# A two-layer kernel's schedule: two lead-in experts moved into scan pairs 0 and 2, totals split, four more pairs summed by DMA, the last norm on VectorE

## What is computed

```python
# layer 0, feed-forward: 8 experts, every token through every expert, weights of the best two
h = gelu(einsum('te,ieh->tih', xf, w1) + b1)          # 128 -> 512, 8 experts
out = einsum('tih,ihe->tie', h, w2) + b2              # 512 -> 128
x = x + gb * sum(out * weights[..., None], axis=1)
# layer 1, attention-like part: a state-space scan, 16 states, 256 channels
dA = exp(dt_t[:, :, None] * A[None])
h = dA * h + (dt_t * xv_t)[:, :, None] * B_t[:, None, :]
y_t = einsum('bdn,bn->bd', h, C_t)                    # sum over the 16 states
x = x + ga * ((y * silu(z)) @ W_out.T)
# layer 1, feed-forward: a linear map by FFT, folded into one 128x128 matrix
x = x + gb * real(ifft(fft(layernorm(x)...) @ w)) + bias
```

## Time and profile before

| | us |
|---|---|
| median of 3 runs (lowest, highest) | 599.6 (598.94, 604.6) |
| the profiled execution, its own time | 605.89 |
| its span in the profile | 603.9 |
| busy: PE, DVE, ACT, POOL | 484.5, 429.1, 341.8, 348.0 |
| lead-in pair -12 to the first scan product | about 165 to 265.77 |
| scan pairs 0 to 31, first to last scan product | 265.77 to 577.64 |

### The profile page before, as it was taken

How to read it: one execution, slowest core, us unless ns; L and a number is a source line. 1 busy time by engine, 2 the same in 40 slices (tenths; PEclk the granted TensorE clock), 3 DMA queues, 4 the chain that set the end, 5 groups by cost and what they waited for, 6 DMA issues and landing times.

```text
span 603.9 us, 6833 instructions
## 1 busy us (share of the span) xinstructions
PE 484.5 (80%) x2346; PEld 337.3 (56%) x2346; DVE 429.1 (71%) x723; ACT 341.8 (57%) x455; POOL 348.0 (58%) x248
## 2 busy tenths in 40 slices
PE   3869867679989999989879979889888397677672
PEld 3457545344578887667666767656757243233231
DVE  4766897964534324059898799997998966987951
ACT  0531443224454655589998999979999255343100
POOL 3214977766432132315597667988487955567443
PEclk9986999979999999999999999999999588888796
DMA  8700000000000000301857655658627511211000
GB/s 292 274 1 0 1 1 1 2 0 0 1 0 2 1 2 0 142 1 46 198 115 151 158 137 141 145 117 207 144 74 171 122 54 53 71 69 35 17 0 18
DMA packets 15010, 44.75 MB, mean 74 GB/s; under 512 B 2240, under 2 KB 7744, under 8 KB 12544
## 3 DMA queue, kind: packets, MB, share of 16 engines
q0 software_dynamic: 2448, 17.83, 14.6%
q1 hardware_dynamic: 11952, 25.57, 12.5%
q10 hardware_dynamic: 576, 0.92, 0.5%
HBM read 25.31 MB, written 1.18 MB: 44 GB/s over the span
## 4 chain that ended last, share of the span: by engine, by line
PE 39%; DVE 28%; ACT 11%; POOL 10%; issue 7%; DMA 4%; ACTq 0%; POOLq 0%; DVEq 0%
PE pO L1219 8%; PE pY L1309 6%; DVE Hs L763 6%; DVE S L658 5%; DVE pCT L750 4%; PE pY L1266 3%; POOL ZS L383 3%; DMA Acc<-ZS 3%; PE pH L1207 3%; DVE pH L657 3%; ACT gel L961 3%; ACT dA L973 2%; PE pH L1209 2%; PE pH L1208 2%; POOL ln_x L353 2%
## 5 line engine op out<-in xcount | busy, mean ns | idle before, releaser
L1219 PEld LDWEIGHTS pO<-w_e,gel 128*128 128x128 f32 x1024 | 122.1, 192 | 13.9 <-issue 8.7
L1219 PE MATMUL pO<-w_e,gel 128*128 128x128 f32 x1024 | 124.7, 276 | 1.2 <-DVE X L734 1.0
L763 DVE TENSOR_TENSOR_SCAN Hs<-dA,HL,pCT 128x512 f32<-128x512 f32 x96 | 117.7, 1267 | 7.4 <-POOL Zev L383 3.7
L961 ACT ACTIVATE gel<-pH,b_e 128x512 f32<-128x512 f32 x128 | 86.1, 687 | 40.0 <-PE pH L1209 39.2
L383 POOL TENSOR_TENSOR ZS<-Hs,Crow 128x1024 f32<-128x1024 f32 x32 | 76.7, 2398 | 42.5 <-DVE Hs L763 42.5
L973 ACT ACTIVATE dA<-dt,a_neg 128x512 f32<-128x512 f32 x128 | 81.8, 710 | 15.8 <-DVE Hs L763 15.6
L750 DVE TENSOR_TENSOR pCT<-u,pB 128x1024 f32<-128x1024 f32 x64 | 78.3, 1224 | 16.8 <-PE pB L1291 15.8
L1207 PE MATMUL pH<-h2h,w_e1h 128*128 128x512 f32 x128 | 57.6, 450 | 21.1 <-ACT gel L961 20.1
L383 POOL TENSOR_TENSOR Zev<-Hs,Crow 128x1024 f32<-128x1024 f32 x26 | 62.5, 2408 | 17.3 <-DVE Hs L763 11.7
L734 DVE SCALAR_TENSOR_TENSOR X<-pO,wts,X 128x128 f32<-128x128 f32 x128 | 35.9, 342 | 42.1 <-PE pO L1219 42.0
L439 POOL TENSOR_TENSOR ZA<-Qsb,S 128x1024 f32<-128x1024 f32 x16 | 38.0, 2373 | 35.0 <-DVE S L658 32.7
(11 more groups left out here) (223 smaller groups left out, 882.8 us busy)
## 6 DMA issues: line engine op xcount, KB each, us to landing
Crow<-c_rows SPq DMA_DIRECT2D x32, 512.0 KB, 4.1
Acc<-ZS POOLq DMA_DIRECT2D x10, 1024.0 KB, 8.8
Acc<-Zev POOLq DMA_DIRECT2D x7, 1024.0 KB, 8.4
w_e<-in_w_e SPq DMA_DIRECT2D x2, 2048.0 KB, 10.6
X<-in_x SPq DMA_DIRECT2D x4, 256.0 KB, 7.4
out<-h2T SPq DMA_DIRECT2D x4, 256.0 KB, 2.5
S<-in_w_mod ACTq DMA_DIRECT2D x2, 384.0 KB, 4.9
w_cx<-in_conv_row SPq DMA_DIRECT2D x1, 512.0 KB, 9.5
```

What stands on the lines that cost most here:

```text
L763: vec.tensor_tensor_scan(Hs[:, 2 * o + d, 0:w], dA[:, 4 * (p % 2) + 2 * o + d, 0:w], pU[:, d, 0:w], HL[:, d, n:n + 1] if c else 0.0, ALU.m ...
L961: nc.scalar.activation(gel[:, n % NG, 0:w], pH[n % 2][:, 0:w], ACT.Gelu_apprx_tanh, bias=b_e1[:, NK * e + k:NK * e + k + 1]).then_inc(s["m ...
L1219: ins = mm(pO[:, j * P:(j + 1) * P], gel[:, n % NG, j * P:(j + 1) * P], w_e2[:, NK * (g % E) + k, :], start=(k == 0 and j == 0), stop=(k = ...
```

## The change

- **Experts.** A table gives the number of experts of each pair. Pairs -4 and -2 have none, pairs 0 and 2 have two. So expert 8 goes from pair -4 to -3, 9 from -3 to -1, 10 and 11 from -2 and -1 to pair 0, 12 from 0 to 1, 13 and 14 from 1 and 2 to pair 2; from expert 15 (pair 3) on nothing moves. The second expert of a pair runs whole after place B; its predecessor's `moe_acc` then stands at the end of the pair on DVE.
- **Sums.** DMA addition now runs to pair 23 (`TOT = 24`), so pairs 20 to 23 are added by DMA, chunk 2's gate is POOL's, and the Acc matmuls go. PE totals only chunk 3.
- **Split totals.** `total(p, o)` adds one half; half 0 comes ahead of place A and half 1 behind `row_b(2p+2)`.
- **Spare products.** `fill(n)` is n matmuls of 128x512 in the free bank pY0 whose result nobody reads: two in pair 20, four in pair 23, four and one in the last norm.
- **Last norm.** The last of the norms has its four multiplications on DVE and not on POOL.

```diff
 AHEAD = 12
+COUNTS = {-4: 0, -2: 0, 0: 2, 2: 2}
-ALONE = (NL * E - AHEAD) // 2 * 2
+EXPERTS = {p: [] for p in range(-AHEAD - 1, NL * NP + 1)}
+for p in range(-AHEAD, NL * NP):
+    g0 = sum(len(e) for e in EXPERTS.values())
+    EXPERTS[p] = list(range(g0, min(g0 + COUNTS.get(p, 1), NL * E)))
+ALONE = max(p for p in EXPERTS if EXPERTS[p]) + 1
+TOT = (ALONE + NP - 1) // NP * NP
...
         def alone(p):
-            return p >= ALONE
+            return p >= TOT
...
-                          ("end", "bias", last), ("mid", "ln_stats", last),
-                          ("A", "ln_turn", last, 2), ("A", "fft", last)):
+                          ("end", "bias", last), ("mid", "ln_last", last), ("A", "fill", 4),
+                          ("A", "ln_turn", last, 2), ("A", "fill", 1), ("A", "fft", last)):
...
+            def ln_last(c):
+                ln_stats(c)
+                vec.wait_ge(s["ln_rstd"], NC + 1)
+                vec.wait_ge(s["ln_tr"], L[0] - 1)
+                for j in range(blocks(c)):
+                    ins = vec.tensor_scalar(ln_x[:, j, :], rows_of(X, c)[:, j, :], ln_mv[:, j, 0:1], ln_rs[:, j:j + 1],
+                                            ALU.subtract, ALU.mult)
+                ins.then_inc(s["ln_xn"], 1)
...
+                free = ALONE <= p < TOT
+                if ALONE < p < NL * NP:
+                    total(p - 1, 0)
+                if free and not any(at == "A" and stage in mine for at, stage, *_ in stages):
+                    fill(2)
                 run(p, stages, "A")
                 if not moe and 0 <= 2 * p + 2 < NL * NS:
                     row_b(2 * p + 2)
-                if 0 < p < NL * NP:
-                    total(p - 1)
+                if ALONE < p < NL * NP:
+                    total(p - 1, 1)
+                if free and not any(at in ("B", "C") and stage in mine for at, stage, *_ in stages):
+                    fill(2)
...
+                for h in EXPERTS[p][1:]:
+                    for k in range(NK):
+                        up(h, k)
+                    for k in range(NK):
+                        down(h, k)
                 run(p, stages, "C")
...
+            def fill(n):
+                pe.wait_ge(s[held[2][0]], held[2][1])
+                warm(pY0, n)
```

More of the change, by code:

```diff
@@ L217, in totals @@
         def totals(p):
-            return p + 1 - ALONE
+            return p + 1 - TOT
         def summed(c):
-            return NP * (c + 1) <= ALONE
+            return NP * (c + 1) <= TOT
         def sums(p):
-            return len([q for q in range(min(p + 1, ALONE)) if q % 2 == p % 2 and q % NP])
+            return len([q for q in range(min(p + 1, TOT)) if q % 2 == p % 2 and q % NP])
         def col(n):
@@ L344, in _, with ln @@
             L = [0]
-            def ln(c):
+            def ln(c, last=False):
                 J = blocks(c)
@@ L368, in output @@
                 part = slice(2 * o, 2 * o + 2)
-                if p >= ALONE + 2:
+                if p >= TOT + 2:
                     Z = [Zev, ZS][p % 2][:, part, 0:w]
@@ L506, in run @@
                 for at, stage, c, *k in stages:
-                    if (at in ("B", "C", "end")) == last and stage in ("ln_stats", "rows", "route", "gate", "bias"):
-                        {"ln_stats": ln, "rows": rows, "route": route, "gate": gate, "bias": bias}[stage](c)
+                    if (at in ("B", "C", "end")) == last and stage in ("ln_stats", "ln_last", "rows", "route", "gate", "bias"):
+                        {"ln_stats": ln, "ln_last": lambda c: ln(c, True), "rows": rows, "route": route, "gate": gate, "bias": bias}[stage](c)
             for p, stages in later_stages():
@@ L793, in run @@
                         continue
-                    if stage in ("ln_stats", "step", "gate", "tail_x"):
-                        {"ln_stats": ln_stats, "step": step, "gate": gate, "tail_x": tail_x}[stage](c)
+                    if stage in ("ln_stats", "ln_last", "step", "gate", "tail_x"):
+                        {"ln_stats": ln_stats, "ln_last": ln_last, "step": step, "gate": gate, "tail_x": tail_x}[stage](c)
                     elif stage in ("route", "weigh", "fft"):
@@ L804, in _ @@
                     scans(2 * p)
-                if 0 < g <= NL * E:
-                    moe_acc(g - 1)
+                for g in EXPERTS.get(p - 1, [])[-1:]:
+                    moe_acc(g)
                 run(p, stages, False)
@@ L810, in _ @@
                     scans(2 * p + 1)
+                for g in EXPERTS[p][:-1]:
+                    moe_acc(g)
                 run(p, stages, True)
@@ L997, in _ @@
                 run(p, stages, "AB")
+                for g in EXPERTS[p][1:]:
+                    hidden(g, range(NK))
                 run(p, stages, "C")
@@ L1223, in pair @@
             def pair(p, stages):
-                g = p + AHEAD
-                moe = 0 <= g < NL * E
+                moe = bool(EXPERTS[p])
+                g = EXPERTS[p][0] if moe else None
                 if moe:
@@ L1337, in _ @@
             mine = {"ln_turn": lambda c, which, b: ln(c, b), "route": route, "turn": turn, "weigh": weigh, "x_part": x_part,
-                    "rows": rows, "dt_part": dt_part, "z_part": z_part, "total": total, "project": project, "fft": fft}
+                    "rows": rows, "dt_part": dt_part, "z_part": z_part, "total": totals_of, "project": project, "fft": fft,
+                    "fill": lambda n, b: fill(n)}
             def run(p, stages, places):
```

47 lines of the change are left out of this document (23 added, 24 removed).

## The result

| | before | after |
|---|---|---|
| median, us (4 runs each, taken together) | 601.12 | 609.93 |
| lowest, highest | 598.94, 604.6 | 608.02, 611.16 |
| ratio after to before, 95% interval | | 1.0139 [1.0094, 1.0183] |
| profiled execution, its span | 605.89, 603.9 | 611.16, 609.1 |

The change makes the kernel 1.4% slower, 8.8 us between the medians. (The ratio is not the quotient of the two medians, which is 1.0147; before was also measured afresh beside the experiments, with medians of 602.03, 602.19 and 602.08, so a difference between two kernels that were not measured together is uncertain by about 1 us.) The profiled execution of before lies 4.8 above its median and that of after 1.2 above, so the two traces differ by 5.3 only. I keep both accounts: the traces say where the time is, the medians how much it is.

A forecast was written before the change was run, and what follows sets the result against it. No single engine bounds it: PE in the lead-in, DVE, ACT and PE nearly level in scan pairs, a serial chain at the end. +6.7 + 2.5 - 0.7 + 1.3 - 3.4 = +6.4 on 599.6 gives 606.0 us, range 597.0 to 611.5.

The forecast's parts named there:

- pair -2 emptied: Lead-in: without its expert, pair -2 shrinks and the first row_b comes 5.7 us sooner, at 259.6 for 265.28.
- pair -4 emptied, time of the norm's chain: Lead-in: nothing in chunk 0's norm chain waits for expert 8, so transposes stay at 237.49; price 0.
- pair 0 doubled: Pair 0: a second expert exceeds PE's idle time and holds up product 3; costs 6.0 us.
- pair 2 doubled: Pair 2: a second expert, behind ACT's two table loads for z, holds up product 7; costs 6.4 us.
- clock in pair -4: Pair -4: idle PE loses its full clock, slowing the work from 237.49 on; +2.5 us, bounds 0 and +3.4.
- tail, with x_part of pair 21: Tail: -0.7 us for the x_part of pair 21, and +1.3 at the last product after the gate wait.
- end: End: the norm's multiplications on DVE give -2.0, transposes and product at full clock -1.4; sum -3.4 us.
- the doubled pairs hide their second expert: Rival, pairs 0 and 2: PE's idle time takes up the second experts; 593.4 us, product 7 before 298; chance 7%.
- the clock holds: Rival: the clock holds in pair -4, or spare products keep it up for pair 21's x_part; 602 to 604; 18%.
- The tail up to the gate: Tail before chunk 2's gate: earlier dt and DMA sums give -4.0, row_b no longer behind a total -0.4, x_part -0.7.
- The gate on POOL: Pair 25: total(24,0) waits for POOL's gate, ending 528.8; products(52) at +5.9 where -4.4 was reached, last product +1.3.
- the gate holds up nobody: Rival, tail: the gate delays nothing, the tail keeps -4.4 and wins 3 more; 600 us; chance 20%.

The follow-up runs named there:

- e3: The changed kernel with only pair -2 emptied and pair 0 doubled; 601.73 us, 0.998 of before.
- e4: The changed kernel with only pair -4 emptied and pair 2 doubled; 608.42 us, 1.0102 of before.
- e7: The changed kernel with 20 spare products in pair -4, 8 ahead of the weights' transpose and 12 behind the bias; 606.9 us, 1.0065 of before.
- e2: The kernel before with only the table of expert counts and the four loops that read it; 612.27 us, 1.0153 of before.
- e8: The changed kernel with the last norm's multiplications back on POOL; 612.24 us, 1.0178 of before.
- e1: The changed kernel with an empty table of counts, so each pair has one expert again; 598.85 us, 0.9932 of before.
- e9: The changed kernel without its spare products in pair 20, pair 23 and the end; 610.31 us, 1.0116 of before.
- e5: The changed kernel with an empty table and both halves of total(24) put off by a pair; 595.02 us, 0.9864 of before.
- e6: The changed kernel, table kept, with both halves of total(24) put off by a pair; 606.3 us, 1.0061 of before.

## Why the prediction was right, and where its terms were off

The prediction was 606.0 us, within 597.0 to 611.5; the result is 609.93, inside the range and 3.9 above. The direction was forecast, but the largest chance, 0.50, stood on a change within 1%, and 0.42 on slower. By its own terms, against the trace of before:

| term | predicted | measured | from |
|---|---|---|---|
| pair -2 emptied | -5.7 | -5.75 | e3, product 0 |
| pair -4 emptied, time of the norm's chain | 0 | 0 | e4, transposes |
| pair 0 doubled | +6.0 | +6.35 | e3, product 0 to 7: +6.7 |
| pair 2 doubled | +6.4 | +6.6 | e4, product 3 to 7 |
| sum of these | +6.7 | +7.54 | e7, product 7 |
| clock in pair -4 | +2.5 | +3.2 (half of it in pair -1) | after against e7 |
| pairs 4 to 19 | 0 | +1.6 | after, product 28 to 29 and the row below |
| tail, with x_part of pair 21 | -0.7 + 1.3 | -2.9 (+1.0 against e2) | after, product 29 to 63 |
| end | -3.4 | -3.45 | last product to last addition |

With the shift of 0.7 that the start of the trace brings, 7.5 + 3.2 + 1.6 - 2.9 - 3.45 - 0.7 = +5.25, the 5.2 between the two spans. That this sum is so near the forecast's +6.4 is partly luck: the terms up to product 29 are 3.1 too low (+12.3 for +9.2), and the slow tail of before's trace hides it.

**The lead-in and the doubled pairs** went as worked out. The step "PE has 1.25 us idle in a pair and a second expert needs 6.6" holds: behind the second experts it is DVE that waits, 3.16, 5.05 and 2.58, for PE. The rival in which the doubled pairs hide their second expert falls: product 7 is at 308.06, and it decided below 298.

**The clock** fell as forecast, and cost 3.2 for 2.5, near the upper bound of 3.4. The size was near by luck as much as by reckoning: in pair -3, where the term stood, it cost 1.6 in this trace (2.6 in e8, 245.02 - 237.18 against e7's 5.28), and the other 1.6, in pair -1, had no term. The rule of the Trainium skill that the prediction drew on ("TensorE: Matmul & The Clock Gate", section "What's actually happening": the throttled state is the default and activity releases it) is borne out by e7, where products without a reader hold the clock at 1.00. The rival "the clock holds" falls.

**The tail up to the gate.** I put -4.0 and -0.4 and -0.7 there, -5.1; from product 29 to 51, e1 has -7.3 and after -7.7 against before. One thing that the sum left out is a wait ahead of those of the earlier trace rows. DVE by time in before and in e1, product 45:

```profile
488.12 1.23 DVE L750 TENSOR_TENSOR pCT<-u,pB 128x1024 f32<-128x1024 f32 x1 [3.39 <-PE pB L1291]
```

```profile
486.98 1.23 DVE L769 TENSOR_TENSOR pCT<-u,pB 128x1024 f32<-128x1024 f32 x1 [1.99 <-PE pB L1325]
```

This wait is for a row_b behind the slow x_part, 6.64 us before, 5.24 in e1, 5.76 in after, 5.05 in e9. But e2, with the tail of before, has 5.26 and a wait of 2.01 too. So its fall is the clock in that one trace of before, not the change. In the changed tail that clock makes no difference further on: e5 has 6.58 there and waits 3.33, yet stands at -7.3 by product 51 like e1, because its next wait, for POOL's Zev, is 1.43 for e1's 2.75. Against e2, which makes -1.98 from product 29 to 51, the change brings -5.3 (e1) and -5.7 (after), and over the whole tail, to product 63, +0.8 and +1.0 where I had +0.6. The ratio of e1 says the same less sharply: it is 4.1 us below before (2.1 to 6.0, from its ratio times 602.03), of which the end is 3.45, and that leaves the tail -0.7 (+1.4 to -2.6). The other five traces with the gate wait (e3, e4, e7, e8, e9) have +0.2 to +0.9 by the same count. So the tail as a whole was sized rightly, as far as single traces can tell; it is before's trace that was long.

**The gate on POOL** was there, with PE idle 9.25 us for a forecast 8 and a jump of 9.4 from product 51 to 52 for a forecast 10.3, and what came back after it was 14.06 - 9.41 = 4.65 for 5.9 - 1.3 = 4.6. Of the 4.65, though, e2 has 1.94 with the tail of before, so the change gave back 2.7. The links of the chain were mis-sized, not misplaced. In e1, whose times have no table in them, like those of this part of the prediction, the gate ends at 522.32 + 2.48 = 524.8 for a forecast 528.8:

```profile
482.00 0.95 POOL L407 DMA_DIRECT2D Acc<-Zev  x1 [0.30 <-POOL Zev L393]
...
489.58 0.88 POOL L407 DMA_DIRECT2D Acc<-ZS  x1 [1.94 <-DMA Acc<-Zev]
...
501.49 0.89 POOL L407 DMA_DIRECT2D Acc<-Zev  x1 [0.73 <-DVE Hs L782]
...
510.48 0.88 POOL L407 DMA_DIRECT2D Acc<-ZS  x1 [1.92 <-DVE Hs L782]
...
517.61 2.34 POOL L393 TENSOR_TENSOR ZS<-Hs,Crow 128x1024 f32<-128x1024 f32 x1 [1.48 <-DMA Acc<-ZS]
```

DMA(21) goes 7.6 after DMA(20), where I took 9.3; DMA(23) so comes 1.7 earlier than the 512.2 that I had; and it frees output(25,0) 7.1 after its issue, not 9.3. The rival "the gate holds up nobody" falls as to the wait, and I had its price wrong: without the wait the kernel is 3.6 (e6) to 3.8 us (e5) faster in the median and not 6 to 8 (the rival's sum has -5 for the tail and the bounds have -7, against the forecast's +1.3), since the projection needs the same gate.

**Pair 14** was not in the sum. The convolution there runs partly at half clock:

```profile
410.48 5.29 PE L1300 MATMUL pY<-h3T,w_cx 128*128 128x512 f32 x8
```

against 3.60 in e8 at 411.06. It is in the traces of after, e3, e4, e6 and e7, and not in those of before, e1, e2, e5, e8 and e9, of which e2, e8 and e9 have the full table. None of the three traces without the table has it. So the table seems to be needed for it but doesn't bring it about by itself; what decides it stays open, and no run was made for it.

**From the trace to the median.** The sum of the traces, +5.3, is less than the +8.8 of the medians because the profiled execution of before was a late one of its kind; the 3.9 us that its tail has over e2's make +9.2. The prediction put its +6.4 on a median of 599.6, which further runs set at 601.1 to 602.2, and that is 1.5 of the 3.9 by which it was low. The other 2.4 are terms that were too small: the table's price (11.1 for 9.2) is 1.9 of them, and within it the doubled pairs (7.54 for 6.7), the clock (3.2 for 2.5) and pair 14, which has no term in the sum. The last 0.5 is less than these medians can tell.

## What to carry to other kernels

An expert that runs beside a serial chain of other engines is free where it stands; before moving work out of a "light" stretch, ask whether that engine was the bound there, and count what its idle time does to the clock of the work behind it, which here lost as much in pair -1 as right behind the hole in pair -3. Moving a block into a pair in which three engines are level costs the block's whole time, here 6.35 to 6.6 us for an expert reckoned at 6.6. When a wait is put in an in-order queue, look for what stands behind it; moving the waiting instruction back is worth only what the next reader of the same result leaves over, here 4 of 9 us. And split a difference by the traces but size it by medians: the one profiled execution can lie 5 us off its kernel's, and a second kernel with the same code in a stretch (here e2's tail) shows where.

## What the runs showed of the hardware that was not expected

- Products whose result nobody reads keep the granted clock at 1.00 and were worth 3.2 us of 610 in one place (e7), 1.4 in another (e9 against after; 0.4 where the norm stayed on POOL, e8 against before), and nothing in a third. PE by time in the kernel after, pair 20 and 21:

```profile
479.47 1.02 PE L1072 MATMUL pY<-X,ident 128*128 128x512 f32 x2
485.18 0.61 PE L1325 MATMUL pB<-ST,sel 96*128 96x512 bf16 x1 [4.69 <-DVE pCT L769]
...
490.75 1.09 PE L1039 MATMUL pH<-ident,ln_x 128*128 128x128 f32 x4 [3.25 <-POOL ln_x L363]
```

The spare products are followed by 4.69 and then 3.25 idle us, and the transposes run at half clock all the same.
- An idle stretch of 3.45 us ahead of 0.63 us of transposes (e8) left these at full clock and put the product 1.2 us behind them at nearly half (1.91 for 1.13). In e9, 4.79 us of idle time put the transposes themselves at half clock (1.09). So the loss can fall on the work after the next, where a look at the first row misses it.
- Kernels that differ only in the tail (after, e8, e9) give a convolution of 3.60 or 5.29 us in pair 14, in one trace of each.
- One accumulating DMA of 1 MB held up the next instruction that waited for it until 7.2 us, 7.6 and 9.3 after its issue in one and the same trace (after's rows at 521.65, 493.22 and 512.38); I had taken one row's 9.3 for all.
